# Two attention heads on two 64-row halves of the matmul array, with their scores in two neighbouring PSUM banks

## The reference, cut to what matters

```python
q = (x @ Wq.T).reshape(B, S, H, hd).transpose(0, 2, 1, 3)
k = (x @ Wk.T).reshape(B, S, H, hd).transpose(0, 2, 1, 3)
v = (x @ Wv.T).reshape(B, S, H, hd).transpose(0, 2, 1, 3)
q = layernorm(q, q_gamma, q_beta)
k = layernorm(k, k_gamma, k_beta)
q = q * cos + rotate_half(q) * sin
k = k * cos + rotate_half(k) * sin
scores = scale * jnp.einsum('bhqd,bhkd->bhqk', q, k)
scores = jnp.where(mask, scores, -jnp.inf)
attn = jax.nn.softmax(scores, axis=-1)
out = jnp.einsum('bhqk,bhkd->bhqd', attn, v)
return out.transpose(0, 2, 1, 3).reshape(B, S, D) @ Wo.T + bo
...
h = jax.nn.silu(h1) * h3
y = jnp.einsum('te,ted->td', combine, jnp.einsum('tei,eid->ted', h, We2) + be2)
```

## Time and profile before

| what | value |
|---|---|
| time, median of 3 runs | 501.55 us (500.71 to 501.96) |
| span of the profiled execution | 499.5 us, 2.05 us under the median |
| PE busy | 411.5 us, 82% |
| DVE busy | 404.1 us, 81% |
| ACT busy | 281.3 us, 56% |
| POOL busy | 201.5 us, 40% |
| chain that ended last | PE 48%, DVE 27%, DMA 9%, issue 6%, POOL 5%, ACT 4% |
| mean granted TensorE clock | 0.909 of 2.4 GHz |

### The profile page before, as it was taken

One profiled execution on the slowest core, in us unless ns is written; L12 is line 12 of the kernel. 1 busy time (PEld: TensorE's weight loads), 2 busy tenths in 40 slices (PEclk: granted clock), 3 DMA queues, 4 the chain that ended last, 5 costly groups with the idle time before them and its releaser, 6 DMA issues.

```text
span 499.5 us, 8243 instructions
## 1 busy us (share of the span) xinstructions
PE 411.5 (82%) x2663; PEld 229.3 (46%) x2663; DVE 404.1 (81%) x966; ACT 281.3 (56%) x627; POOL 201.5 (40%) x319
## 2 busy tenths in 40 slices
PE   1631169799999997886999996999999999886995
PEld 0310134344435344462556554655364444674784
DVE  6988999799999989669998893797989951478465
ACT  1412015374659781566465873356566899674674
POOL 7427413242021303766364444443340222485353
PEclk9965569899999997988899997899999999999889
DMA  4805404400000026047038009000000000800530
GB/s 131 148 0 79 47 0 62 68 4 1 1 3 0 2 65 108 0 58 70 1 48 84 1 10 185 0 2 0 2 18 7 1 3 4 168 3 0 128 65 22
DMA packets 29821, 19.98 MB, mean 40 GB/s; under 512 B 8850, under 2 KB 29619, under 8 KB 29779
## 3 DMA queue, kind: packets, MB, share of 16 engines
q1 hardware_dynamic: 29106, 18.81, 22.4%
q0 software_dynamic: 144, 0.39, 0.6%
q10 hardware_dynamic: 528, 0.26, 0.2%
HBM read 11.86 MB, written 1.18 MB: 26 GB/s over the span
## 4 chain that ended last, share of the span: by engine, by line
PE 48%; DVE 27%; DMA 9%; issue 6%; POOL 5%; ACT 4%; SPq 1%; POOLq 0%; ACTq 0%; DVEq 0%
PE psum L718 10%; PE psum L762 10%; PE psum L744 9%; DMA comb_b<-combine_scratch 7%; PE psum L811 5%; DVE mx_diag L1152 4%; DVE roped L1115 3%; PE psum L712 3%; PE psum L686 3%; PE psum L799 2%; POOL mh L1042 2%; POOL mv L559 2%; PE psum L800 2%; DVE seed L1058 2%; DVE roped L1129 2%
## 5 line engine op out<-in xcount | busy, mean ns | idle before, releaser
L872 ACT ACTIVATE probs<-psum 128x512 f32<-128x512 f32 x288 | 152.7, 604 | 78.9 <-PE psum L744 56.6
L718 PE MATMUL psum<-k_st,q_st 126*128 126x512 bf16 (+3 forms) x384 | 110.5, 348 | 1.5 <-DVE mx_full L1152 1.1
L1031 POOL TENSOR_SCALAR_AFFINE_SELECT probs<-probs 128x256 f32<-128x256 f32 (+1 forms) x160 | 58.7, 369 | 125.8 <-ACT probs L872 121.9
L1152 DVE TENSOR_REDUCE mx_diag<-psum 128x2 f32<-128x256 f32 (+2 forms) x192 | 103.1, 591 | 7.7 <-PE psum L718 6.7
L744 PE MATMUL psum<-q_st,k_st 128*128 128x512 bf16 (+3 forms) x384 | 97.9, 334 | 3.2 <-DMA q_st<-maxT 2.1
L1152 DVE TENSOR_REDUCE mx_full<-psum 128x1 f32<-128x512 f32 x128 | 80.1, 679 | 12.4 <-PE psum L718 11.9
L762 PE MATMUL psum<-probs,v_ones 128*16 128x512 f32 (+3 forms) x768 | 78.2, 495 | 0.2 <-ACT o_raw L939 0.2
L1042 POOL TENSOR_TENSOR mh<-mh,mv 128x256 f32<-128x256 f32 x72 | 55.6, 778 | 52.7 <-DVE mh L1239 42.5
L712 PE MATMUL psum<-causal_bf,ident_bf 128*128 128x128 bf16 (+1 forms) x192 | 49.0, 256 | 29.8 <-DMA k_st<-parts 25.9
L811 PE MATMUL psum<-w,mh 128*128 128x128 f32 x288 | 50.4, 308 | 18.8 <-POOL mh L1042 18.7
L1239 DVE SCALAR_TENSOR_TENSOR mh<-mh,mu 128x256 f32<-128x256 f32 x72 | 39.7, 562 | 27.8 <-ACT mh L919 27.4
(11 more groups left out here) (138 smaller groups left out, 453.9 us busy)
## 6 DMA issues: line engine op xcount, KB each, us to landing
comb_b<-combine_scratch SPq DMA_DIRECT2D x16, 512.0 KB, 9.2
q_st<-parts SPq DMA_DIRECT2D x48, 64.0 KB
k_st<-parts SPq DMA_DIRECT2D x21, 128.0 KB
w<-in_We SPq DMA_DIRECT2D x3, 512.0 KB
out<-xs SPq DMA_DIRECT2D x4, 256.0 KB, 6.6
xs<-in_x SPq DMA_DIRECT2D x3, 256.0 KB, 5.2
k_st<-parts POOLq DMA_DIRECT2D x3, 128.0 KB, 5.1
xs<-in_x ACTq DMA_DIRECT2D x1, 256.0 KB, 3.5
```

The source lines that it names most:

```text
L718: last = pe.matmul(w[:, i * keys:(i + 1) * keys], q_st[0:KM, x % 2, m, par, q0:q0 + P], k_st[0:KM, b, m, k0:k0 + keys], start=(what == "fu ...
L872: act.activation(probs[:, n % P_RING, :], bank(ST_BANK + n % ST_RING), ACT.Exp, scale=SCALE).then_inc(exp_done, 1)
L1031: pool.affine_select(out=v, in_=v, compare_op=ALU.is_ge, fill=0.0, base=0, pattern=[[0, v.shape[1]], [1, P]], channel_multiplier=-1).then_ ...
L1152: dve.tensor_reduce(dst[:, qt, j // 2:j // 2 + nh, j % 2], w, AX.X, ALU.max).then_inc(max_free, 1)
```

## The change

Each head of a pair gets its own 64 rows of the array: six terms of 8 rows, 14 rows of zeros, and the two rows of ones or of the maximum as rows 62 and 63 of its half. The even head lies in rows 0 to 63, the odd one in 64 to 127, in `q_st` and `k_st` alike. `q_st` no longer has a copy for each head. Each product is now two matmuls, one on each half, into two neighbouring banks (`wpair`), issued one behind the other. One DVE reduction reads both banks (up to 1024 elements), one ACT exponential reads both (1024 columns). POOL masks both heads together.

Banks are handed out in pairs (`PAIR_BANKS`): scores take (0,1) or (2,3), maxima (4,5), then (2,3), then (0,1); single stages take 6, 5, 4, 3 or 2. The sum of `pv` moves to bank 7, the experts' sum to 6. There are six buffers of two banks for the probabilities. A Q copy fills 16 rows instead of 8, so a chunk has 6 copies instead of 12; the row maxima take two DMAs instead of one; the ones come from DRAM by two DMAs for each sequence. The planner has new durations and new windows, so the order of all engines changes. The number of matmuls and their columns are the same.

```diff
-N_STACK = 3 * len(TERMS_Q)
+N_STACK = 2 * len(TERMS_Q)
-KM = P - 2
+ROWS = P // 2
+KM = ROWS - 2
-ST_RING, P_RING, MOE_RING = 3, 10, 4
-ST_BANK, ACC_BANK, WORK_BANKS, Y_BANK = 0, 3, (4, 5, 6), 7
+P_RING, MOE_RING = 6, 4
+ACC_BANK, Y_BANK = 7, 6
+PAIR_BANKS = {"scores": ((0, 1), (2, 3)), "max": ((4, 5), (2, 3), (0, 1))}
+SINGLE_BANKS = (6, 5, 4, 3, 2)
...
+        def wpair(kind, arg):
+            first = FILL_BANK[FILL[kind, arg]][0]
+            return psum[:, first:first + 2, :]
...
-                    for par in range(2):
-                        row = 16 * t + 8 * par
-                        engine.dma_start(q_st[row:row + 8, x % 2, :, par, :],
-                                     parts[64 * par:64 * par + 64, which, part, :]).then_inc(done, 16)
+                    engine.dma_start(dst[t::HD], parts[:, which, part, :]).then_inc(done, 16)
...
-                    sp.dma_start(q_st[KM:P, x % 2, 2 * g:2 * g + 2, :, :],
-                                 maxT[:, arg % 2, :]).then_inc(maxrow_in[arg % 2], 16)
+                    for par in range(2):
+                        sp.dma_start(q_st[ROWS * par + KM:ROWS * (par + 1), x % 2, 2 * g:2 * g + 2, :],
+                                     maxT[4 * par:4 * par + 4, arg % 2, :]).then_inc(maxrow_in[arg % 2], 16)
...
-                for i, j in enumerate(heads):
-                    par, m = j % 2, 2 * g + j // 2
-                    q0 = qt * P
-                    last = pe.matmul(w[:, i * keys:(i + 1) * keys], q_st[0:KM, x % 2, m, par, q0:q0 + P],
-                                     k_st[0:KM, b, m, k0:k0 + keys],
-                                     start=(what == "full"), stop=True, skip_group_check=True)
+                for i, m in enumerate(pairs):
+                    for par in range(2):
+                        r = slice(ROWS * par, ROWS * par + KM)
+                        last = pe.matmul(w[:, par, i * keys:(i + 1) * keys], q_st[r, x % 2, 2 * g + m, q0:q0 + P],
+                                         k_st[r, b, 2 * g + m, k0:k0 + keys],
+                                         start=(what == "full"), stop=True, skip_group_check=True)
...
-                for j, kt, col, cols, q0 in bursts_of(c)[k][i][0]:
-                    par, m = j % 2, 2 * g + j // 2
-                    last = pe.matmul(w[:, col:col + cols], k_st[:, b, m, kt * P:(kt + 1) * P],
-                                     q_st[:, x % 2, m, par, q0:q0 + cols],
-                                     start=True, stop=True)
+                for m, kt, col, cols, q0 in bursts_of(c)[k][0][i]:
+                    for par in range(2):
+                        last = pe.matmul(w[:, par, col:col + cols], k_st[rows(par), b, 2 * g + m, kt * P:(kt + 1) * P],
+                                         q_st[rows(par), x % 2, 2 * g + m, q0:q0 + cols],
+                                         start=True, stop=True)
...
-                act.activation(probs[:, n % P_RING, :], bank(ST_BANK + n % ST_RING), ACT.Exp,
+                act.activation(probs[:, n % P_RING, :, :], wpair("scores", (s, i)), ACT.Exp,
                                scale=SCALE).then_inc(exp_done, 1)
...
-                dve.tensor_reduce(dst[:, qt, j // 2:j // 2 + nh, j % 2], w, AX.X, ALU.max).then_inc(max_free, 1)
+                dve.tensor_reduce(dst[:, qt, :, pairs[0]:pairs[0] + nm], w, AX.X, ALU.max).then_inc(max_free, 1)
```

210 lines of the change are left out of this document (105 added, 105 removed).

## The result

The changed kernel took 515.42 us (median of 4 runs, 513.09 to 518.85), the kernel before 501.75 us on the same chip. The ratio is 1.0252, 95% interval 1.0197 to 1.0307: 2.5% slower. The prediction was 488 us, range 467 to 507. The span of the profiled execution went from 499.5 to 512.9 us.

A forecast was written before the change was run, and what follows sets the result against it. The prediction took DVE as the nearer bound, PE as second. Its terms, -14 + 9 - 4 - 2 - 2 = -13, took the 499.5 us span to 486.5, and with 2.05 us for the median to 488 us, range 467 to 507.

The forecast's parts named there:

- What bounds the kernel: Over the whole span: DVE the nearer bound, PE second; 8.7 us of DVE's waits are for a late PE.
- the rival's 471 us: Long stretch and end: PE was the bound after all, so a lighter PE gives 471 us; chance 0.20.
- Reductions, -14: DVE's maxima: 160 fewer reductions save 14 us, bounds 11 and 24, at 0.071 to 0.148 us each.
- Refilling a pair, +9: Maxima on DVE: 17 reductions wait some 0.55 us each for PE to refill their pair; 9 us lost, bounds 0 and 16.
- PE columns, -4: Scores and maxima on PE: overlapping halves, less changes of shape, save 4 us on the path, bounds 0 and 8.7.
- the prediction's third case: Diagonal units on PE: halves don't overlap or shape changes cost more; half of 33 us shows, 508 us; chance 0.16.
- Exponentials, -2: ACT after the last maximum: exponentials of 1024 columns instead of 512 save 2 us, bounds 0 and 4.
- DMA, -2: Chunk 1's Q copies: fewer issues take away 2 us of waiting for the row maxima's DMA.
- the masks: POOL: 160 masks become 112 instructions, 58.7 us of POOL time falls to about 52; nothing on the path.
- The order, "I count them even": End against long stretch: four bursts (4 x 2.4 us) leave the end, 8 us of DVE work return; net nothing.
- The clock: PE: a lighter load lowers its granted clock, 500 us if the mean falls from 0.91 to under 0.85; chance 0.17.

The follow-up runs named there:

- before_bias64: The kernel before, order unchanged, with the causal bias of diagonal units multiplied from rows 0 to 63 alone: 532.66 us, ratio 1.0587.
- full_rows: The changed kernel, order unchanged, with scores and products of maxima on all 128 rows, the halves one after the other: 523.5 us, ratio 1.0402.
- half_order_bias128: The changed kernel, every instruction kept, with other planner tables setting the order: 493.89 us, ratio 0.9811 to the kernel before.

## Why the prediction was wrong, step by step

**What bounds the kernel.** "DVE is the nearer bound, PE the second": half right. before_bias64 shows PE as near: 33 us more of PE made 29.5 us. That does not bear out the rival's 471 us, since PE's busy time in the long stretch fell by only 2.9 us.

**Reductions, -14.** The unit price came out as costed, 1.14 us each in a row. Of the 23.6 us by which DVE's busy time fell only about half is the reductions': undoing the edit brings back 11.4 us in one order and 10.4 in the other, the 0.071 us each of the lower end and not the 0.148 of the upper one. On the path it is 5.7 us in the change's order and 7.4 in the good one, about half of the 14. The term was mis-sized by taking more than the lower end and all of it as on the path.

**Refilling a pair, +9.** Not measured by itself. The waits of DVE for L720 grew by 22.3 us, more than twice that, but those of 1.6 to 2.1 us are a wait for PE's turn, not for a refill of 0.55 us. The "0.20 us after its releaser" was misread: the bracket in the earlier trace rows tells how long PE had stood idle, not how late it started. Its size is near all the same; a reduction that ends at 225.08 us is followed by PE at 225.22, 0.14 us later. That these waits are as long in the order that is 22 us faster says that the term is no measure of the loss.

**PE columns, -4.** The halves overlap and bring 7.5 us in one order and 6.1 in the other, net of all the changes of shape that they need, since full_rows has none of these within the diagonal units either. That is within the term's bounds of 0 and 8.7. Without the changes within the diagonal units it would be 4.3 to 4.5 more (the edit that shows this also takes away half of the bias columns). The price of one change, 0.10 to 0.11 us, was right. The Trainium skill (TensorEngine Tiling (Array Packing), Key Properties) says that changing the tiling mode drains the TensorE, and these 0.10 to 0.11 us agree with it. What was too low is the price of PE's load when it is added: half in the prediction's third case, nearly all in before_bias64. That PE's busy time fell by 15.6 us and not by 25 to 34 goes with its clock, 0.876 instead of 0.909, which makes the same matmuls some 3.7% or 15 us longer (a rough estimate from the page's 395.9 us).

**Exponentials, -2.** 1.4 us in one order and 3.8 in the other, neither clearly apart from 2. **DMA, -2**, and the masks: not tried apart. In the trace of the changed kernel PE waits for the row maxima's DMA for 0.6 us in all instead of the 2.1 of the earlier trace rows, as the term had it.

**The order, "I count them even".** This is the step that failed. The order was weighed by two items, four bursts moved behind the last maximum (9.6 us) and 8 us of DVE work back into the long stretch. The end did become shorter, by 12.5 us. But what was moved was larger, 15.2 us of DVE (56.5 us of DVE work behind the last maximum before, 41.3 now), and it was never asked how well the lists of the two engines fit together in the long stretch. They fit worse: 29 us more of idle PE and 32 more of idle DVE than before. The same instructions in another order take 22 us less. The forecast was missed by 27 us (515.42 against 488), so this one step is most of it; in the good order the changed kernel takes 493.89 us, inside the forecast's own 478 to 497. The lists in the section on the change showed before any run that maxima now stood one pair at a time between bursts, which should have been a warning to cost the order. It isn't shown to be the cost itself, since the good order has that too.

**The clock.** The rival put the point at 0.85; it was 0.876, and the profiled run of half_order_bias128 has 0.878 at 495.29 us. It adds to PE's time but is not the cause of the 22 us.

**What stays open.** What was shown by experiment is that the order as a whole takes 22 us and that the waits for the combine weights are not the reason. The order was found by a search and not derived, and only one search was tried for the kernel before, so which entry of the tables matters, and what the best order of each kernel would be, isn't known. The traces say where the idle time lies and not which of it costs. The three instruction terms measured 7.4, 6.1 and 3.8 us in the good order, some 17, and the whole is 9.5 faster than the kernel before, of which 8.4 are the shorter waits for the combine weights (17 - 8.5). If these add up, some 16 us are given back by the pairs of banks and by what is left of the order against the kernel before; these weren't told apart.

The fastest kernel here that leaves out no wait for the combine weights is half_planned, the change with half of the bias rows left out and other tables: 488.65 us, 2.8% below the kernel before.

## What to carry to other kernels

When a change comes with a new order, cost the order as a term of its own, and don't settle it by counting what moved across one mark. Laying the two fullest engines side by side in stretches shows where idle time has grown, but compare that with a faster order before calling a stretch the cause: the most striking one here was the same in both. If a tuned kernel gets slower while every engine gets less to do, try its new instructions in another order before giving the change up. Where two engines are both over 80% busy, don't take load that is added to one of them for hidden: 33 us added to PE cost 29.5 here. In the changed kernel, with PE at 77%, load taken away came back as a third (24.5 us of PE gave 8.5); whether the direction or the room on PE makes this difference wasn't tried.

## What the runs showed of the hardware

- 192 matmuls moved from 128 rows to 64 made a kernel 5.9% slower, 0.11 us for each change between a tile of 64 rows and one of 128, at 2.4 GHz; about the same as the 0.10 and 0.13 us around `pv`'s column tiles.
- Not sure before: two row tiles run at once, six matmuls of 512 columns in 0.82 us, what three took on all rows.
- An instruction of DVE or ACT that reads two neighbouring banks pays nothing for the second: 1.215 us for 1024 elements on DVE against 1.213 from SBUF, and 3.75 us for four in a row on ACT against 5.19 for ten of half the size.
